# A four-layer graph network on one core: GpSimd's order at the start, a table load between two stages, and the elu ends of the last attention group moved

## The chip, the cores and the metric

The kernel runs on one core of one Trainium2 chip. The metric is device time in microseconds (us) of one execution. It is launched once and computes everything on the core. Engines are TensorE (PE), VectorE (DVE), ScalarE (ACT), GpSimd (POOL) and SyncE (SP), which issues most of the transfers.

## The reference, cut to what matters

There are N = 1250 nodes of 1024 features and E = 20000 edges (src, dst, edge_weight), sorted by dst. Four layers are applied, each as x = x + layer(relu(layernorm(x))):

```
edge_index = stack([src, dst])
x = x + L0(h)   # x1 = h @ W1 + b1 (1024 -> 512); four gated rounds:
                # deg = in-degree; dis = max(deg, 1) ** -0.5
                # alpha = tanh(x_i @ gw[:512] + x_j @ gw[512:] + gb)
                # out += segment_sum(dis[row] * dis[col] * alpha * x_j, col)
                # result is concat([x1, out])
x = x + L1(h)   # W = zeros(1024, 1024).at[row, col].add(edge_weight); h @ W.T + bias
x = x + L2(h)   # graph convolution with self loops: relu(A_norm (h @ W) + b)
x = x + L3(h)   # h = h @ W; e = exp(-leaky_relu(al[src] + ar[dst]))
                # h' = segment_sum(e * h[dst], src) / (rowsum + 1e-5)
                # elu(h')
```

## The kernel before

Nodes are padded to 1280 and worked in T = 10 tiles of 128. Matrix products run in fp32r; each left or right operand is split into a high part and a remainder (`_hi` by ScalarE, `_lo` by VectorE), and TensorE does three products (hi x hi, hi x lo, lo x hi).

**Layer 0, first part (0 to 123 us).** For every tile, `x1_pe` multiplies with W1. Between the steps of this product TensorE builds the matrix of edge counts and the matrix of edge weights: edges are picked into windows of five nodes with one-hot matrices (`pick_edges`), then `cells` (VectorE) makes one-hot operands for 25 groups, `cells_pe` multiplies them and `take_cells` (ScalarE) copies them out. `place_pe`, `place_act` and `place_dve` say which group is handled at which of four places in a tile; these orders are written out by hand. `transpose_pe` turns the normalised input, `transposed_act` and `transposed_dve` split it into `hT_hi` and `hT_lo`.

GpSimd makes the layernorm factor of a pair of tiles with `scale_pool(i)`, six instructions on 128x2 values (L532 to L542), because the power function there keeps ScalarE's table alone. It also splits the edge weights into three bf16 parts (`ew_part`, five instructions on 80x250 values, L844 to L852), which `pick_edges` needs for its last six products (L1787). ScalarE's `place_bias(0)` (L1008) writes the bias times the factor into the bank of the first product; TensorE's first product waits for it. ScalarE also makes `w1_hi` for eight rows of blocks (L1029) and VectorE `w1_lo` (L1411). The edges' ends and weights are then blended by VectorE (L1309 to L1336), and ScalarE's `widen_parts` (L1045, `ew_ids`) makes them ready for `cells`.

**From layer 0's first part to the gated rounds (112 to 125 us).** VectorE computes `norm` from the degrees; ScalarE takes its root (`norm_root`, L1093), VectorE makes `dis` from it (L1493 to L1501). A dummy Tanh on ScalarE (L1095) stands behind the root. `gates(t, ..)` (L1391, L1394, VectorE) makes the two gate values of a tile. `spread_u` (L1866, TensorE) puts `u` on all partitions. Then for every tile s of a half: `tanh` (ACT, L1110), `mask_of` (DVE, L1508), `mask_hi_of` (ACT, L1115), `mask_rest` (DVE, L1513), and 15 products (L1972 to L1974) on TensorE. `g_split` (ACT, L1099) and `g_rest` (DVE, L1399) split g. `take_x1(t)` (L996) copies x1 of tile t.

**Layers 1 and 2 (404 to 730 us)** are not touched.

**Layer 3, attention (845 us to the end).** Five groups of two destination tiles; for each group ten steps s: `logits`, `att_of` (L1688), `att_rest` (L1693) on VectorE, `exps` and `att_hi_of` on ScalarE, `sum_e` (L944 to L950) on GpSimd, 12 products on TensorE (`gat_step`, L2052). `att_rest(s)` waits for `sum_e(s)`. The group's result is finished during the next group: `gat_take` and `elu_act` on ScalarE, `elu_start` at s == 4 and `elu_end` (L1714, L1718) at s 7 and 8 on VectorE. `elu_end` adds the residual in `xres[j]` and leaves the result there.

SyncE has one queue in this stage, in this order for each of two buffers: wait for `gat_added`, store `xres[j]` to the output (L796), wait until the store has landed, load the next residual tile into the same buffer (L792):

```
def store3(i, b):
    settled(sp, gat_added, 2 * i + b + 1)
    sp.dma_start(out[rows(2 * i + b), :], xres[b][:, :]).then_inc(gat_stored[b], 16)
    settled(sp, gat_stored[b], 16 * (i + 1))
with sp.Fori(0, HT - 1) as i:
    for b in range(2):
        store3(i, b)
        load3(i + 1, b)
```

So the residuals of tiles 8 and 9 are loaded only when tiles 6 and 7 have been finished and stored. The last tile is finished in two halves of 512 columns; L1764 and L1767 are the second half's last instructions on VectorE, L1277 and L1278 ScalarE's, and L810 stores both halves.

Of the kernel before, what the change touches and what calls it, by code (L numbers as in the profile page):

```python
# [59 lines left out]
SLOTS = 5  # L60
TANH_LEAD = 3
AL_FIRST = T - 2
SCALES_AHEAD = {0: 1, 1: 2, 4: 3, 7: 4}
LAST_SUMS = (2, 3, 4, 0, 1)
EARLY = 3
TAIL = 3
# [9 lines left out]
def build_program(nc, x, src, dst, edge_weight, w1, b1, gate_w, gate_b, bias1, w2, b2, w3, att, out):  # L76
# [738 lines left out]
    def _(pool):  # L815
# [19 lines left out]

        pool.wait_ge(src_landed, 16)
        nc.gpsimd.tensor_copy(src_h[0:EDGE_ROWS, :, :], src_rows[0:EDGE_ROWS, :, :]).then_inc(src_ready, 1)
        pool.wait_ge(firsts_done, 1)
        scale_pool(pool, 0)
        pool.wait_ge(ew_landed, 16)  # L840
        ew_whole = ew_rows[0:EDGE_ROWS, :, :].rearrange("p t c -> p (t c)")
        part = [ew_part[0:EDGE_ROWS, n, :] for n in range(3)]
# [8 lines left out]
        pool.wait_ge(parts_chain, 4)  # L851
        nc.gpsimd.tensor_copy(part[2], left_over[1]).then_inc(parts_chain, 1)  # L852

        for a in range(T):
            if a in SCALES_AHEAD:
                scale_pool(pool, SCALES_AHEAD[a])
            pool.wait_ge(count_row_ready, a + 1)
            pool.dma_start(count_dram[a * P:(a + 1) * P, :], count_row[a % 2][:, :]).then_inc(count_stored[a % 2], 16)
            if a < WT_TILES:
                pool.wait_ge(weights_copied, a + 1)  # L860
                pool.dma_start(wt_dram[a * P:(a + 1) * P, :], weight_row[a % 2][:, :]).then_inc(weights_stored[a % 2], 16)
# [98 lines left out]
    def _(act):  # L960
# [50 lines left out]
        def place_act(t, place):  # L1011

            for n in groups_at(t, place, 0):
                take_cells(n)
            for a in tiles_behind(t, place, 1):
                if a < WT_TILES:
                    take_weight_rows(a)
            for a in tiles_behind(t, place, 2):
                take_count_rows(a)
# [2 lines left out]
        transposed_act(act, d, 0, 0)  # L1022
        h_act(act, d, 0, 1)
        for k in range(KT):
            if k == 2:
                place_bias(0)
            if k % 2 == 0:
                act.wait_ge(w_landed[k // 2], 16)
            nc.scalar.activation(w1_hi[:, k, :], w1_raw[:, k, :], ACT.Copy).then_inc(w_hi_ready, 1)  # L1029
# [18 lines left out]
        for t in range(T):  # L1048
            if t + 1 < T:
                transposed_act(act, d, (t + 1) // 2, (t + 1) % 2)  # L1050
            place_act(t, 0)
            if t > 0:
                take_x1(t - 1)
            place_act(t, 1)
            if t + 2 < T:
                h_act(act, d, (t + 2) // 2, t % 2)
            if t + 1 < T and t % 2 == 0:
                place_bias(t + 1)
            if t == 0:
                widen_rows()  # L1060
                widen_parts()
            if t == FIRST_STEP:
                act.wait_ge(complete_ready, 1)
                whole = act.value_load(complete[0:1, 0:1], min_val=0, max_val=1)
            place_act(t, 2)
            if t + 1 < T and t % 2 == 1:
                place_bias(t + 1)
            place_act(t, 3)

        with act.If(whole == 0):  # L1070
            act.wait_ge(count_row_ready, T)
# [19 lines left out]

        act.wait_ge(norm_chain, 2)
        nc.scalar.activation(norm_root[:, :, :], norm[:, :, :], ACT.Sqrt).then_inc(norm_root_ready, 1)  # L1093

        nc.scalar.activation(rden[:, 0, 0:1], zeros[:, 0:1], ACT.Tanh).then_inc(tanh_idle, 1)  # L1095


        def g_split(t):
# [13 lines left out]
        def mask_hi_of(q, s):  # L1112
            k = s % SLOTS
            act.wait_ge(mask_ready, T * q + s + 1)
            nc.scalar.activation(mask_hi[k][:, :], mask[k][:, :], ACT.Copy).then_inc(mask_hi_ready, 1)  # L1115
# [35 lines left out]
        act.wait_ge(product_read[0], 1)  # L1151
        g_split(0)
        act.wait_ge(count_stored[0], 16 * HT)
        tanh(0, 0, 0, 1)
        mask_hi_of(0, 0)
        act.wait_ge(product_read[1], 1)
        g_split(1)
        act.wait_ge(product_ready[0], HT)
# [109 lines left out]
        with act.Fori(1, GROUPS - 1) as grp:  # L1268
            attention_act(grp, range(T), False, False)
        attention_act(GROUPS - 1, range(T), False, True)  # L1270
        gat_take(T - 2, 0)
        elu_act(T - 2, 0)
        gat_take(T - 1, 1, slice(0, HID))
        elu_act(T - 1, 1, slice(0, HID))
        end = slice(HID, D)
# [6 lines left out]
    def _(dve):  # L1282
# [130 lines left out]
        for t in range(T):  # L1413
# [22 lines left out]
                whole = dve.value_load(complete[0:1, 0:1], min_val=0, max_val=1)  # L1436
            if t == T - 2:
                gates(4, 4)
            place_dve(t, 2)
            place_dve(t, 3)  # L1440
            if t == T - 3:
# [126 lines left out]
                if h == 1 and s >= HT:  # L1568
                    g_rest(s - HT, T * nxt + s - HT)

        gates(5, 5)
        dve.wait_ge(counts_copied, CELL_GROUPS)
        mask_of(0, 0, 0)
        g_rest(0, 0)
# [145 lines left out]
        def attention_dve(grp, steps, first, last):  # L1720

            for s in steps:
                if s < T - 2:
                    logits(grp, s + 2)
                elif not last:
                    if s == T - 2 and not first:
                        dve.wait_ge(al_all_ready, 2)
                    logits(grp + 1, s + 2 - T)
                if s < T - 1:
                    att_of(grp, s + 1)  # L1730
                elif not last:
                    att_of(grp + 1, 0)
                att_rest(grp, s)
                if not first and s == 4:
                    for j in range(GRP):
                        elu_start(GRP * (grp - 1) + j, j)
                if not first and s in (7, 8):
                    elu_end(GRP * (grp - 1) + s - 7, grp - 1, s - 7)

        def attention_start():  # L1740
            dve.wait_ge(al_ready, AL_FIRST)
# [380 lines left out]
```

## Time and profile before

| | |
|---|---|
| time, median of 3 runs | 1001.96 us (1000.94 to 1003.04) |
| the profiled execution | 1001.58 us, its span 1000.0 us |
| TensorE busy | 977.4 us, 98% of the span |
| VectorE, ScalarE, GpSimd busy | 668.7, 430.9, 140.4 us |
| chain that ended last | PE 91%, DVE 5%, ACT 2%, issue 1%, POOL 1% |

The span is the time in which the profiler saw the core work; 1.58 us of the profiled execution lie around it. The chain that ended last is followed back from the last instruction, each time to what released the instruction. Starts are us from the beginning of the span.

### The profile page before, as it was taken

The page shows a single profiled execution, that of the slowest core. Times are in us where ns is not written, and L with a number is a line of the kernel's source. Part 1 is how long each engine was busy: PE and PEld are TensorE (multiplying, and loading weights), DVE is VectorE, ACT ScalarE, POOL GpSimd, SP SyncE. Part 2 cuts the span into 40 slices and gives each one's busy share as a digit, 9 for nine tenths or more (in the row PEclk, how much of TensorE's full clock was granted, in tenths as well). Part 3 has the DMA queues.
Part 4 walks back from the last instruction along what each step waited for, and adds up shares of the span by engine and source line. Part 5 has one row for each costly group of instructions (what it writes and reads, how often), then busy time and mean ns, then how long its engine had stood idle before and what let it go on. Part 6 is the DMA issues. An engine that isn't in the chain of part 4 may idle for free.

```text
span 1000.0 us, 14720 instructions
## 1 busy us (share of the span) xinstructions
PE 977.4 (98%) x5170; PEld 809.6 (81%) x5170; DVE 668.7 (67%) x1221; ACT 430.9 (43%) x650; POOL 140.4 (14%) x191
## 2 busy tenths in 40 slices
PE   5999999999999999999999999999999999999997
PEld 3788788888888888888888888888888888888886
DVE  7877888788778879354485343216446664988886
ACT  5688865554543646112242322233222232445543
POOL 3022500000000010232221000000110000333331
PEclk9999999999999999999999999999999999999999
DMA  7256580000000014745433111243451230101223
GB/s 251 101 177 222 136 255 1 1 22 0 0 21 0 0 12 104 178 171 188 180 124 116 42 42 43 77 155 106 156 180 69 69 121 0 43 22 64 84 84 122
DMA packets 27326, 93.42 MB, mean 93 GB/s; under 512 B 3530, under 2 KB 3530, under 8 KB 27136
## 3 DMA queue, kind: packets, MB, share of 16 engines
q1 hardware_dynamic: 16400, 58.07, 16.5%
q0 software_dynamic: 10880, 34.74, 11.4%
q8 instruction: 29, 0.48, 0.2%
q14 instruction: 17, 0.14, 0.0%
HBM read 64.48 MB, written 33.56 MB: 98 GB/s over the span
## 4 chain that ended last, share of the span: by engine, by line
PE 91%; DVE 5%; ACT 2%; issue 1%; POOL 1%; DMA 0%; ACTq 0%; DVEq 0%; POOLq 0%
PE ps L592 32%; PE ps L2052 11%; PE ps L1972 9%; PE ps L1974 9%; PE ps L1973 9%; PE ps L2025 5%; PE ps L2024 5%; PE ps L575 3%; PE ps L1895 1%; PE ps L1897 1%; PE ps L1896 1%; PE ps L1866 1%; PE ps L1822 1%; PE ps L1825 1%; PE ps L1838 1%
## 5 line engine op out<-in xcount | busy, mean ns | idle before, releaser
L1972 PE MATMUL ps<-g_hi,mask_hi 128*128 128x512 f32 x400 | 157.4, 394 | 2.1 <-DVE mask_lo L1513 2.1
L1974 PE MATMUL ps<-g_hi,mask_lo 128*128 128x512 f32 x400 | 155.9, 390 | 0.0
L1973 PE MATMUL ps<-g_lo,mask_hi 128*128 128x512 f32 x400 | 155.7, 389 | 0.0
L558 ACT ACTIVATE hT_hi<-ps 128x1024 fp32r<-128x1024 f32 x40 | 41.0, 1025 | 200.3 <-PE ps L575 200.3
L592 PE MATMUL ps<-w_hi,hT_hi 128*128 128x512 f32 x320 | 126.4, 395 | 0.0
L592 PE MATMUL ps<-w_lo,hT_hi 128*128 128x512 f32 x320 | 124.7, 390 | 0.0
L2052 PE MATMUL ps<-y_all,att_hi 128*128 128x512 f32 x400 | 110.0, 393 | 1.5 <-DVE att_lo L1693 1.5
L1110 ACT ACTIVATE mask<-ps,v 128x640 f32<-128x640 f32 x80 | 63.4, 793 | 111.2 <-PE ps L1974 52.9
L592 PE MATMUL ps<-w_hi,hT_lo 128*128 128x512 f32 x320 | 98.6, 389 | 0.0
L1972 PEld LDWEIGHTS ps<-g_hi,mask_hi 128*128 128x128 f32 x400 | 75.1, 188 | 20.4 <-DVE mask_lo L1513 3.3
L2052 PEld LDWEIGHTS ps<-y_all,att_hi 128*128 128x128 f32 x400 | 74.0, 188 | 17.3 <-DVE att_lo L1693 1.5
L1974 PEld LDWEIGHTS ps<-g_hi,mask_lo 128*128 128x128 f32 x400 | 75.1, 188 | 16.0
L1973 PEld LDWEIGHTS ps<-g_lo,mask_hi 128*128 128x128 f32 x400 | 75.1, 188 | 15.1
L565 DVE TENSOR_TENSOR hT_lo<-ps,hT_hi 128x1024 fp32r<-128x1024 f32 x40 | 48.9, 1222 | 46.3 <-ACT hT_hi L558 46.3
L1508 DVE TENSOR_TENSOR mask<-mask,countT 128x640 f32<-128x640 f32 x80 | 65.5, 819 | 14.2 <-ACT mask L1110 14.2
L592 PEld LDWEIGHTS ps<-w_hi,hT_lo 128*128 128x128 f32 x320 | 60.1, 188 | 12.8
L592 PEld LDWEIGHTS ps<-w_lo,hT_hi 128*128 128x128 f32 x320 | 60.2, 188 | 11.8
L592 PEld LDWEIGHTS ps<-w_hi,hT_hi 128*128 128x128 f32 x320 | 60.1, 188 | 11.9
L1513 DVE TENSOR_TENSOR mask_lo<-mask,mask_hi 128x640 fp32r<-128x640 f32 x80 | 65.3, 818 | 0.4 <-ACT mask_hi L1115 0.3
L1115 ACT ACTIVATE mask_hi<-mask 128x640 fp32r<-128x640 f32 x80 | 58.8, 735 | 15.3 <-DVE mask L1508 15.0
L592 PE MATMUL ps<-wt_hi,hT_hi 128*128 128x512 f32 x160 | 63.3, 396 | 0.0
L2052 PE MATMUL ps<-y_all,att_lo 128*128 128x512 f32 x200 | 63.3, 390 | 0.0
(203 smaller groups left out, 1839.2 us busy)
## 6 DMA issues: line engine op xcount, KB each, us to landing
xin<-x_after SPq DMA_DIRECT2D x30, 512.0 KB, 3.3
xres<-x_after POOLq DMA_DIRECT2D x20, 512.0 KB, 4.2
x_after<-xres POOLq DMA_DIRECT2D x20, 512.0 KB, 3.0
w_raw<-in_L_gnn_W SPq DMA_DIRECT2D x8, 1024.0 KB, 7.2
x_after<-g POOLq DMA_DIRECT2D x20, 256.0 KB, 7.4
xres<-x_after SPq DMA_DIRECT2D x10, 512.0 KB, 3.4
xin<-in_x SPq DMA_DIRECT2D x9, 512.0 KB, 3.4
out_x<-xres SPq DMA_DIRECT2D x9, 512.0 KB, 2.7
```

Source lines behind the costliest of these rows:

```text
L565: nc.vector.tensor_tensor(hT_lo[b][:, :, :].rearrange("p k m -> p (k m)"), TRANSPOSED, hT_hi[b][:, :, :].rearrange("p k m -> p (k m)").bit ...
L592: last = nc.tensor.matmul(PRODUCT[d.n][b][:, half * BANK:(half + 1) * BANK], left[:, k, :], right[:, k, half * BANK:(half + 1) * BANK], st ...
L1110: nc.scalar.activation(mask[k][:, :], U_ALL, ACT.Tanh, bias=v[:, s:s + 1]).then_inc(tanh_ready, 1)
L1115: nc.scalar.activation(mask_hi[k][:, :], mask[k][:, :], ACT.Copy).then_inc(mask_hi_ready, 1)
L1508: nc.vector.tensor_tensor(mask[k][:, :], mask[k][:, :], countT[:, s, h * HALF:(h + 1) * HALF], ALU.mult).then_inc(mask_ready, 1)
L1513: nc.vector.tensor_tensor(mask_lo[k][:, :], mask[k][:, :], mask_hi[k][:, :].bitcast(F32), ALU.subtract).then_inc(mask_lo_ready, 1)
L1972: nc.tensor.matmul(SUMS[dd], mask_hi[k][:, cols], g_hi[:, s, :], start=(s == 0), stop=False)
L1973: nc.tensor.matmul(SUMS[dd], mask_hi[k][:, cols], g_lo[:, s, :], start=False, stop=False)
L1974: last = nc.tensor.matmul(SUMS[dd], mask_lo[k][:, cols], g_hi[:, s, :], start=False, stop=(s == T - 1))
L2024: nc.tensor.matmul(out_n, left, y_hi[s][:, n * BANK:(n + 1) * BANK], start=(s == 0), stop=False)
L2025: last = nc.tensor.matmul(out_n, left, y_lo[s][:, n * BANK:(n + 1) * BANK], start=False, stop=(s == T - 1))
L2052: last = nc.tensor.matmul(AGG[j][:, n * BANK:(n + 1) * BANK], left, right[:, n * BANK:(n + 1) * BANK], start=(s == 0 and len(rights) == 2 ...
```

## The change

Five things are changed.

- On GpSimd the five instructions on the edge weights now stand ahead of `scale_pool(0)`. On ScalarE `place_bias(0)` moves from ahead of the third block of `w1_hi` to ahead of the seventh.
- ScalarE runs a dummy Sqrt in step t = 8 of the first part, behind `place_act(8, 3)`. The dummy Tanh behind the root is removed. (That `place_act(t, 0)` changes sides with `take_x1(t - 1)` at t = 9 moves no instruction: no group and no tile falls on that place.)
- ScalarE's `mask_hi_of(0, 0)` comes ahead of `tanh(0, 0, 0, 1)`.
- VectorE's `gates(5, 5)` moves from behind `dis` to step t = 8, ahead of `norm`.
- In the last attention group VectorE runs both `elu_end` behind the ten steps and no longer at s 7 and 8. ScalarE's last `gat_take`s wait for `gat_added`, since they overwrite `gat_sums`.

```
-        pool.wait_ge(firsts_done, 1)
-        scale_pool(pool, 0)
         pool.wait_ge(ew_landed, 16)
...
         nc.gpsimd.tensor_copy(part[2], left_over[1]).then_inc(parts_chain, 1)
+        pool.wait_ge(firsts_done, 1)
+        scale_pool(pool, 0)
...
         for k in range(KT):
-            if k == 2:
+            if k == 6:
                 place_bias(0)
...
             place_act(t, 3)
+            if t == T - 2:
+                nc.scalar.activation(rden[:, 0, 1:2], zeros[:, 0:1], ACT.Sqrt).then_inc(tanh_idle, 1)
...
         nc.scalar.activation(norm_root[:, :, :], norm[:, :, :], ACT.Sqrt).then_inc(norm_root_ready, 1)
-        nc.scalar.activation(rden[:, 0, 0:1], zeros[:, 0:1], ACT.Tanh).then_inc(tanh_idle, 1)
...
+        mask_hi_of(0, 0)
         tanh(0, 0, 0, 1)
-        mask_hi_of(0, 0)
...
+        act.wait_ge(gat_added, T - GRP - 1)
         gat_take(T - 2, 0)
         elu_act(T - 2, 0)
+        act.wait_ge(gat_added, T - GRP)
         gat_take(T - 1, 1, slice(0, HID))
...
             if t == T - 2:
                 gates(4, 4)
+                gates(5, 5)
...
-        gates(5, 5)
         dve.wait_ge(counts_copied, CELL_GROUPS)
         mask_of(0, 0, 0)
...
-                if not first and s in (7, 8):
+                if not first and not last and s in (7, 8):
                     elu_end(GRP * (grp - 1) + s - 7, grp - 1, s - 7)
+            if last:
+                for j in range(GRP):
+                    elu_end(GRP * (grp - 1) + j, grp - 1, j)
```

## Rows read from the trace of the kernel before

**Rows 1.** Timeline of GpSimd, 9 to 17 us: start, duration, what [idle before, releaser]

```profile
9.22 0.73 POOL L532 TENSOR_TENSOR rough<-variance,minus_half 128x2 f32<-128x2 f32 x1 [1.72 <-DVE variance L506]
...
11.27 0.39 POOL L844 CAST ew_part<-ew_rows 80x250 bf16<-80x250 f32 x1
...
12.46 2.00 POOL L848 CAST ew_part<-ew_rest 80x250 bf16<-80x250 f32 x1
...
15.55 0.73 POOL L852 CAST ew_part<-ew_rest 80x250 bf16<-80x250 f32 x1
```

**Rows 2.** The transfer of the edge weights: issue, and us from issue to landing

```profile
L687 SPq DMA_DIRECT2D ew_rows<-in_edge_weight x1: 441/441/441, 3.4 to 3.4; - x1
...
DMA to landing us min/median/max: 6.6/6.6/6.6
```

**Rows 3.** Timeline of ScalarE, 12 to 29 us

```profile
12.82 0.68 ACT L1008 ACTIVATE ps<-b_all,bias_scale 128x512 f32<-128x512 f32 x1
...
13.43 3.21 ACT L1029 ACTIVATE w_hi<-w_raw 128x512 fp32r<-128x512 f32 x6
...
27.90 1.46 ACT L1045 ACTIVATE ew_ids<-edges 125x1500 bf16<-125x1500 f32 x1
```

**Rows 4.** Timeline of VectorE, 12 to 32 us

```profile
12.93 5.71 DVE L1411 TENSOR_TENSOR w_lo<-w_raw,w_hi 128x512 fp32r<-128x512 f32 x8
...
21.90 1.23 DVE L565 TENSOR_TENSOR hT_lo<-ps,hT_hi 128x1024 fp32r<-128x1024 f32 x1 [0.39 <-ACT hT_hi L558]
...
26.11 1.08 DVE L1336 COPY_PREDICATED edges<-here,ps 125x250 f32<-125x250 int32 x3
...
30.31 1.22 DVE L565 TENSOR_TENSOR hT_lo<-ps,hT_hi 128x1024 fp32r<-128x1024 f32 x1 [1.32 <-ACT hT_hi L558]
```

**Rows 5.** Timeline of ScalarE: the first table load, and 116 to 121 us

```profile
1.03 1.28 ACT L551 ACT_TABLE_LOAD   x1 [1.03 <-PEq L2112]
...
116.48 0.69 ACT L996 ACTIVATE g<-ps,scale 128x512 f32<-128x512 f32 x1 [1.49 <-PE ps L1897]
117.19 1.28 ACT L1093 ACT_TABLE_LOAD   x1
...
120.12 0.78 ACT L1110 ACTIVATE mask<-ps,v 128x640 f32<-128x640 f32 x1
```

**Rows 6.** ScalarE's queue: the waits ahead of the first tanhs, ns, 100 to 130 us

```profile
L1109 ACTq EVENT_SEMAPHORE  x6: 17/28/2115, 116.8 to 129.8; - x6
```

**Rows 7.** Timeline of VectorE, 118 to 127 us

```profile
118.73 0.28 DVE L1493 RECIPROCAL dis<-norm_root 128x20 f32<-128x20 f32 x1 [3.31 <-ACT norm_root L1093]
...
119.91 0.69 DVE L1391 CUSTOM_DVE_ANT_0 gate_scratch<-g,gw 128x512 f32<-128x512 f32 x1
...
125.44 0.82 DVE L1513 TENSOR_TENSOR mask_lo<-mask,mask_hi 128x640 fp32r<-128x640 f32 x1 [0.27 <-ACT mask_hi L1115]
```

**Rows 8.** Timeline of TensorE: the first product of the gated rounds

```profile
123.92 0.47 PE L1972 MATMUL ps<-g_hi,mask_hi 128*128 128x512 f32 x1 [0.88 <-DVE mask_lo L1513]
```

**Rows 9.** Timeline of TensorE in the last attention group

```profile
984.06 1.19 PE L2052 MATMUL ps<-y_all,att_hi 128*128 128x512 f32 x4 [1.12 <-DVE att_lo L1693]
```

**Rows 10.** Timeline of VectorE, 993 to 997 us

```profile
993.44 0.69 DVE L1714 SCALAR_TENSOR_TENSOR elu_neg<-elu_neg,xres 128x512 f32<-128x512 f32 x1 [0.77 <-ACT elu_neg L1236]
...
995.88 0.69 DVE L1764 SCALAR_TENSOR_TENSOR elu_neg<-elu_neg,xres 128x512 f32<-128x512 f32 x1 [0.69 <-ACT elu_neg L1277]
```

**Rows 11.** Timeline of GpSimd in the last attention group

```profile
975.37 0.74 POOL L946 TENSOR_TENSOR e_part<-e_part,att_e 128x256 f32<-128x256 f32 x1 [0.89 <-DVE att_e L1688]
```

**Rows 12.** Timeline of SyncE's queue, 980 to 989 us

```profile
980.43 0.35 SPq L796 DMA_DIRECT2D out_x<-xres  x1
983.33 0.34 SPq L792 DMA_DIRECT2D xres<-x_after  x1
...
988.83 0.34 SPq L792 DMA_DIRECT2D xres<-x_after  x1
```

**Rows 13.** Landing of the six loads of L792, 925 to 1000 us

```profile
DMA to landing us min/median/max: 3.1/3.4/4.0
```

More of the change, by code:

```diff
@@ L62 @@
 AL_FIRST = T - 2
-SCALES_AHEAD = {0: 1, 1: 2, 4: 3, 7: 4}
+SCALES_AHEAD = {0: (1,), 1: (2,), 4: (3,), 7: (4,)}
 LAST_SUMS = (2, 3, 4, 0, 1)
@@ L837, in _ @@
         nc.gpsimd.tensor_copy(src_h[0:EDGE_ROWS, :, :], src_rows[0:EDGE_ROWS, :, :]).then_inc(src_ready, 1)
-        pool.wait_ge(firsts_done, 1)
-        scale_pool(pool, 0)
         pool.wait_ge(ew_landed, 16)
@@ L852, in _ @@
         nc.gpsimd.tensor_copy(part[2], left_over[1]).then_inc(parts_chain, 1)
+        pool.wait_ge(firsts_done, 1)
+        scale_pool(pool, 0)
         for a in range(T):
-            if a in SCALES_AHEAD:
-                scale_pool(pool, SCALES_AHEAD[a])
+            for i in SCALES_AHEAD.get(a, ()):
+                scale_pool(pool, i)
             pool.wait_ge(count_row_ready, a + 1)
@@ L1024, in _ @@
         for k in range(KT):
-            if k == 2:
+            if k == 6:
                 place_bias(0)
@@ L1050, in _ @@
                 transposed_act(act, d, (t + 1) // 2, (t + 1) % 2)
-            place_act(t, 0)
+            if t < T - 1:
+                place_act(t, 0)
             if t > 0:
                 take_x1(t - 1)
+            if t == T - 1:
+                place_act(t, 0)
             place_act(t, 1)
@@ L1068, in _ @@
             place_act(t, 3)
+            if t == T - 2:
+                nc.scalar.activation(rden[:, 0, 1:2], zeros[:, 0:1], ACT.Sqrt).then_inc(tanh_idle, 1)
         with act.If(whole == 0):
@@ L1093, in _ @@
         nc.scalar.activation(norm_root[:, :, :], norm[:, :, :], ACT.Sqrt).then_inc(norm_root_ready, 1)
-        nc.scalar.activation(rden[:, 0, 0:1], zeros[:, 0:1], ACT.Tanh).then_inc(tanh_idle, 1)
         def g_split(t):
@@ L1153, in _ @@
         act.wait_ge(count_stored[0], 16 * HT)
+        mask_hi_of(0, 0)
         tanh(0, 0, 0, 1)
-        mask_hi_of(0, 0)
         act.wait_ge(product_read[1], 1)
@@ L1270, in _ @@
         attention_act(GROUPS - 1, range(T), False, True)
+        act.wait_ge(gat_added, T - GRP - 1)
         gat_take(T - 2, 0)
         elu_act(T - 2, 0)
+        act.wait_ge(gat_added, T - GRP)
         gat_take(T - 1, 1, slice(0, HID))
@@ L1438, in _ @@
                 gates(4, 4)
+                gates(5, 5)
             place_dve(t, 2)
@@ L1569, in half_dve @@
                     g_rest(s - HT, T * nxt + s - HT)
-        gates(5, 5)
         dve.wait_ge(counts_copied, CELL_GROUPS)
@@ L1736, in attention_dve @@
                         elu_start(GRP * (grp - 1) + j, j)
-                if not first and s in (7, 8):
+                if not first and not last and s in (7, 8):
                     elu_end(GRP * (grp - 1) + s - 7, grp - 1, s - 7)
+            if last:
+                for j in range(GRP):
+                    elu_end(GRP * (grp - 1) + j, grp - 1, j)
         def attention_start():
```

## The prediction

> **What bounds the kernel.** I read the page first. TensorE is busy for 98% of the span and makes nine tenths of the chain that ended last, so an edit pays only where TensorE or that chain waits for what is edited. I then read the chain in order of time. It leaves TensorE in three places, and the change touches these three: the start, up to about 43 us, where it runs over GpSimd, ScalarE and VectorE; the step into the gated rounds at 117 to 124 us; and the last attention group. For each I read the timelines of all engines. The reader should look in [rows 1, 3, 4] for who waits for whom at the start, in [rows 5 to 8] for the 0.88 us in which TensorE is idle before the first gated product, and in [rows 9 to 13] for its 1.12 us in the last group and for the store-and-load chain of SyncE beside it. Middle layers are unchanged and a shift at one place is carried to the end, since TensorE is the bound between them.
>
> **A. The start.** GpSimd makes the factor from 9.22 to 11.27 (2.05 us) and the parts from 11.27 to 16.28 (5.01 us) [rows 1]. The parts can't start before the weights have landed, at 3.4 + 6.6 = 10.0 us [rows 2], so they start 1.2 us earlier and not 2.05. A cast costs 0.39 alone, 0.73 beside VectorE's `w_lo` and once 2.00, when it met the start of that series [rows 1, 4]. With all three casts at 0.39 the five instructions take 5.01 - 1.61 - 0.34 = 3.06 us; done at 13.1. If the last cast, which now falls on 12.4 to 12.5, meets the same 2.0 us, they are done at 14.7. The factor follows: 2.05 us alone, and with 0.34 more for each of six instructions beside `w_lo` 4.1 us. I call its end S. At the ends S = 13.1 + 2.05 = 15.2 and 14.7 + 4.1 = 18.8. I take 17.4: parts done at 13.9, halfway, and 3.5 us for the factor, nearer to the contended row because `w_lo` runs until at least 16.6 (six of 0.62 from 12.93).
>
> What waits for S: `place_bias(0)` now stands ahead of the last two of `w1_hi`. Behind S come the bias (13.43 - 12.82 = 0.61), two `w1_hi` (3.21 / 6 = 0.535 each), one `w1_lo` (about 0.68), and some 0.1 between engines [rows 3, 4]: `w1_lo` ends at S + 2.5. It ended at 18.64 before, so VectorE is late by S - 16.1. Queued behind it on VectorE are the next tile's statistics, the blends and `hT_lo(1)`. Two slacks take something back: 0.39 us of idle ahead of `hT_lo(1)`, and 27.90 - 27.19 = 0.71 us by which the blended weights were ready before ScalarE came to widen them, because it had been held by a bank that TensorE opens; TensorE's earlier picks remove that hold [rows 3, 4]. From there `ew_ids`, `hT_hi(2)` and `hT_lo(2)` follow one another, and VectorE waited 1.32 us for this [rows 4], then ran without a gap into the 43 us mark. So the shift is S - 16.1 - 1.1 = S - 17.2, and no less than -1.1. With S = 17.4 it is **+0.2**; the bounds are -1.1 and +1.6.
>
> A rule of the Trainium skill bears here (SBUF — State Buffer, "Who interferes with whom"): VectorE with two SBUF inputs and a reading GpSimd exclude each other for a whole instruction. The casts of 0.39, 0.73 and 2.00 us agree in kind. By this rule each small instruction would wait for the end of a `w_lo`, some 4 us for the factor, and the sum would be about 0.6 us higher.
>
> **B. Into the gated rounds.** Two table loads stand between `take_x1(8)` and the first tanh: 117.19 to 120.12 [rows 5]. The Sqrt load moves into ScalarE's idle time ahead of 116.48, 1.49 us long; load and dummy take 1.28 + 0.2 = 1.48. That is covered, by a hair; each 0.1 us more would delay `take_x1(8)` by as much. The root then runs at 117.2 and `dis` comes 1.3 us earlier. `gates(5, 5)`, 1.4 us, now stands ahead of `norm`: VectorE was idle 3.31 us waiting for the root [rows 7], of which the load is 1.28 and the rest, 2.0, covers it. Where does the Tanh load go? The queue waits for the spread u from 116.8 for 2.115 us, to 118.9 [rows 6]. The very first load ran at 1.03 us [rows 5], ahead of its activation's wait for statistics of an input that was only being issued then. If this load goes ahead of its waits too, it runs from 117.4 to 118.7 and is hidden, and the first tanh starts at 118.9 instead of 120.12. From there tanh 0.7, `mask_of` 0.75 (no gates ahead of it), `mask_hi` 0.7 (no tanh ahead of it), `mask_lo` 0.8: ready at 122.1. But TensorE is in the last x1 product until 123.92 - 0.88 = 123.04 [rows 8], and nothing moves that. So 1.9 us of earlier masks are worth **-0.9**. The next step keeps it: `take_x1(9)` waits for the same product's end and stands ahead of `mask_hi(1)`, so it too comes 0.9 earlier. Bounds: -0.9, and +0.3 (the third rival).
>
> A second rule speaks against this edit: ScalarE: Activation LUTs, "What ACT_TABLE_LOAD costs", puts a switch at 1.28 us of load and 1.38 us of drain. The trace has two loads, a root and a dummy in 2.93 us [rows 5], which two such switches would not fit into. By the rule the load would reach 1.2 us beyond the idle time and the sum would be about 0.8 us higher.
>
> **C. The end.** TensorE waits 1.12 us for `att_lo` of step 9, because VectorE runs two `elu_end` between steps 7 and 9 [rows 9]. With them behind, the operand is ready long before: -1.1 for TensorE's end. But what is late next is the transfers. `elu_end(6)` now waits for `att_rest(9)`, which waits for two sums on GpSimd, 0.74 each and some 0.3 between [rows 11]: 2 x 1.05 + 0.35 = 2.4 us later; free of GpSimd's reads it is some 0.4 faster. So the store of tile 6 goes from 980.43 to 982.4. Its buffer is loaded 2.9 us later, the other buffer's load follows 5.5 us behind that (983.33, 988.83 in [rows 12]), so at 990.8; it lands 3.1 to 4.0 us later [rows 13], at 993.9 to 994.8. The first half of the last tile needs it; it ran at 993.44 and would be ready at 992.3. VectorE's last instructions had 0.69 us of idle at 995.88 [rows 10], so a landing at L moves the end by L - 993.44 - 0.69: at 994.5, **+0.4**. Bounds: -1.1, if a load waits only for a lone store of 2.9 us and no landing is late, and +0.8, a 4.0 landing with 0.1 to wake. ScalarE's new wait for `gat_added` of tile 6 (982.2) is over before the last step's products, which start at 982.9 and which it needs anyway: no cost.
>
> **Sum.** +0.2 - 0.9 + 0.4 = -0.3 against the profiled execution's own 1001.58 (span 1000.0 and 1.58 around it): 1001.3. The median of the runs is 0.4 above that execution, so 1001.6 to 1001.7; I give 1001.6.
>
> **Rivals.**
> 1. *The last load is in time.* For it: it was so in [rows 12] with the store 2 us earlier, and the loads spread by 0.9 us. Against: SyncE issues one after the other. C = -1.1: total -1.8, 1000.2; with a factor at its earliest (A = -1.1) -3.1, 998.9.
> 2. *The factor becomes the bound (slower than before).* GpSimd's six small instructions each wait out a `w_lo`, place: `place_bias(0)`, S = 18.8. For it: the 2.00 us cast. Against: `w_lo` runs dry by 17 us, and GpSimd is then alone. A = +1.6: total +1.1, 1003.1. Beyond S = 17.7 the whole change is slower than before.
> 3. *The Tanh load stands behind its wait.* For it: this activation has two waits and the one at 1.03 us had one. Then it runs 118.9 to 120.2, tanh is not earlier; the first product is 0.6 earlier by order alone, but `mask_hi(1)`, now behind two tanhs and `take_x1(9)`, ends at 125.7 against 125.4 [rows 7], and VectorE sets the pace there. B = +0.1: total +0.7, 1002.7.
> 4. *The preload doesn't do what it says*, since a branch lies between it and the root and the table is loaded again, or it costs more than its 1.49 us: B about 0: +0.6, 1002.6.
>
> **Chances.** Forecast 0.42, first rival 0.2 (a quarter of it with the early factor), second 0.13, third 0.15, fourth 0.1. Bounds together: -1.1 - 0.9 - 1.1 = -3.1 and +1.6 + 0.3 + 0.8 = +2.7; with the median, 998.9 and 1004.7. The range 999.2 to 1003.6 leaves out only joint extremes. 0.2% is 2.0 us, about what a measurement of this kernel can tell from no change. Only the first rival's early part and the better half of its rest pass it downwards: 0.15; the second with a late landing upwards: 0.06; within 0.2%: 0.79.
>
> **What would show it.** A: `ew_part` starts near 10.05, `bias_scale` ends near 17.4, `hT_lo(2)` near 30.5. B: one table load near 115.0, one near 117.4, no idle of TensorE ahead of L1972, which starts 0.9 earlier relative to A's shift. C: no idle of TensorE in the last group, the second load of L792 near 990.8 and VectorE's L1714 on 512 columns waiting for it. Wrong would be: a factor done before 16, a Tanh load at 118.9, or a residual that lands before 993.

## The result: 1004.3 us, 0.2% slower, where 1001.6 was forecast

The changed kernel takes 1004.30 us (median of 17 runs, 1002.83 to 1005.97) beside 1002.14 us for the kernel before on the same chip; the ratio is 1.0019, with a 95% interval of 1.0012 to 1.0026. That is 2.2 us slower, at the bound of 2.0 us that the prediction called measurable, above its range (to 1003.6). The prediction gave 0.79 to a change within 0.2% and 0.06 to a slower kernel; the measured change lies on the border of the two, the ratio just inside and the difference of the medians just outside. The profiled execution took 1004.52 us, with a span of 1003.0.

The span was followed at marks that both kernels have. Each line gives the start of one instruction before and after:

| mark | before | after | shift | gained or lost since the last |
|---|---|---|---|---|
| `hT_lo(2)` on VectorE (end of A) | 30.31 | 32.18 | +1.87 | +1.87 |
| first gated product on TensorE | 123.92 | 125.80 | +1.88 | 0.0 |
| second spread of u on TensorE (end of B) | 148.23 | 150.78 | +2.55 | +0.67 |
| last group's first row sums on TensorE | 963.88 | 966.47 | +2.59 | +0.04 |
| last product of TensorE | 994.66 | 995.83 | +1.17 | -1.42 |
| last instruction of VectorE (end of C) | 996.60 | 999.63 | +3.03 | +1.86 |

So in the profiled executions A cost 1.87 where +0.2 stood in the sum, B cost 0.67 where -0.9 stood, and C cost 3.03 - 2.59 = 0.44, where +0.4 stood. (The first mark is known less well than its digits say: in the five profiled executions of kernels that keep the old start, `b_alone` to `best1` below, it lies between 29.58 and 31.00.) Between the marks of B and C nothing moved, as the prediction had it.

**The start.** GpSimd's timeline in the changed kernel, 10 to 19 us, which answers to [rows 1]:

```profile
10.64 0.39 POOL L842 CAST ew_part<-ew_rows 80x250 bf16<-80x250 f32 x1 [2.10 <-DMA ew_rows<-in_edge_weight]
...
11.84 0.39 POOL L846 CAST ew_part<-ew_rest 80x250 bf16<-80x250 f32 x1
...
13.00 3.91 POOL L850 CAST ew_part<-ew_rest 80x250 bf16<-80x250 f32 x1
16.88 0.73 POOL L532 TENSOR_TENSOR rough<-variance,minus_half 128x2 f32<-128x2 f32 x1
17.68 0.19 POOL L534 TENSOR_TENSOR square<-rough 128x2 f32<-128x2 f32 x1
...
18.79 0.20 POOL L542 TENSOR_TENSOR bias_scale<-scale,variance 128x2 f32<-128x2 f32 x1
```

VectorE's timeline beside it, 12 to 33 us, which answers to [rows 4]:

```profile
12.97 3.69 DVE L1416 TENSOR_TENSOR w_lo<-w_raw,w_hi 128x512 fp32r<-128x512 f32 x6
20.38 1.29 DVE L1416 TENSOR_TENSOR w_lo<-w_raw,w_hi 128x512 fp32r<-128x512 f32 x2 [3.73 <-ACT w_hi L1029]
...
32.18 1.23 DVE L565 TENSOR_TENSOR hT_lo<-ps,hT_hi 128x1024 fp32r<-128x1024 f32 x1 [0.68 <-ACT hT_hi L558]
```

And the bias on ScalarE's timeline, which answers to [rows 3]:

```profile
19.11 0.69 ACT L1008 ACTIVATE ps<-b_all,bias_scale 128x512 f32<-128x512 f32 x1 [3.36 <-POOL bias_scale L542]
```

Read the three together. The weights' parts do start early, but the third cast takes 3.91 us instead of the 0.39 of the two before it: it begins 0.03 us behind the first `w_lo` and ends 0.25 us behind the sixth. So the parts are done at 16.91, later than before (16.28), and the factor comes behind them, at 18.99. ScalarE waits 3.36 us for it ahead of the seventh `w1_hi`, and VectorE 3.73 us for that one.

**Into the gated rounds.** ScalarE's timeline, 116 to 123 us, answers to [rows 5], and the line under it, from its queue (count: min/median/max ns of waiting), to [rows 6]:

```profile
116.95 1.28 ACT L1073 ACT_TABLE_LOAD   x1
118.24 0.20 ACT L1073 ACTIVATE rden<-zeros 128x1 f32<-128x1 bf16 x1
118.40 0.69 ACT L996 ACTIVATE g<-ps,scale 128x512 f32<-128x512 f32 x1
118.99 0.21 ACT L1098 ACTIVATE norm_root<-norm 128x20 f32<-128x20 f32 x1
120.91 1.28 ACT L1113 ACT_TABLE_LOAD   x1 [1.71 <-issue]
122.21 0.80 ACT L1113 ACTIVATE mask<-ps,v 128x640 f32<-128x640 f32 x1
...
L1112 ACTq EVENT_SEMAPHORE  x5: 17/17/1982, 118.9 to 129.6; - x5
```

The Sqrt load is hidden: `take_x1(8)` starts at 118.40, and 116.48 plus the shift of 1.88 would be 118.36. The Tanh load isn't: ScalarE stands idle for 1.71 us while its queue waits for the spread of u from 118.9 for 1.98 us, and the table is loaded only then. TensorE's timeline at the first gated products, which answers to [rows 8]:

```profile
125.80 0.47 PE L1980 MATMUL ps<-g_hi,mask_hi 128*128 128x512 f32 x1 [0.83 <-DVE mask_lo L1519]
...
133.26 0.47 PE L1980 MATMUL ps<-g_hi,mask_hi 128*128 128x512 f32 x1 [0.42 <-DVE mask_lo L1519]
```

The idle of 0.88 us has become 0.83, and another of 0.42 stands behind it. The way from `take_x1(8)` to the first gated product is as long as before (7.40 us against 7.44), so the missed load took away a gain and lost nothing. The 0.67 us are lost behind that product: from it to the second spread of u it takes 24.98 us, before 24.31. Two lines show where, the first from ScalarE's timeline, the second from VectorE's:

```profile
124.05 0.74 ACT L1118 ACTIVATE mask_hi<-mask 128x640 fp32r<-128x640 f32 x1 [0.44 <-DVE mask L1514]
128.01 0.82 DVE L1519 TENSOR_TENSOR mask_lo<-mask,mask_hi 128x640 fp32r<-128x640 f32 x1 [0.96 <-ACT mask_hi L1118]
```

With `mask_hi_of(0, 0)` ahead of the second tanh, ScalarE stands idle for 0.44 us until `mask_of` is done; in the kernel before it made that tanh in the meantime. Now two tanhs and not one stand between the first `mask_hi` and the second, which start 3.18 us apart instead of 2.51. So the second `mask_lo` starts 2.21 us behind the first gated product and no longer 1.52 (125.44 in [rows 7]).

**The end.** In the last group TensorE no longer waits for `att_lo`; the 1.12 us of [rows 9] are gone. The view of waits (total us, times, longest) of the whole execution has one such wait left, and it ends at 864.96, in the first group:

```profile
PE ps L2060 <- DVE att_lo L1698: 0.4, 1, 0.4
```

VectorE's timeline, 992 to 1001 us, answers to [rows 10]:

```profile
992.14 1.23 DVE L1719 SCALAR_TENSOR_TENSOR elu_neg<-elu_neg,xres 128x1024 f32<-128x1024 f32 x1 [3.09 <-DMA xres<-x_after]
...
997.12 0.69 DVE L1719 SCALAR_TENSOR_TENSOR elu_neg<-elu_neg,xres 128x512 f32<-128x512 f32 x1 [1.71 <-DMA xres<-x_after]
...
999.63 0.69 DVE L1775 TENSOR_TENSOR xres<-elu_neg,gat_sums 128x512 f32<-128x512 f32 x1
```

SyncE's timeline, 985 to 994 us, answers to [rows 12]:

```profile
985.20 0.35 SPq L796 DMA_DIRECT2D out_x<-xres  x1
988.09 0.34 SPq L792 DMA_DIRECT2D xres<-x_after  x1
988.77 0.35 SPq L796 DMA_DIRECT2D out_x<-xres  x1
993.55 0.34 SPq L792 DMA_DIRECT2D xres<-x_after  x1
```

The load that must wait for the store goes out at 988.09, the next one 5.46 us behind it, and VectorE, free since TensorE's products came earlier, waits 3.09 and 1.71 us for the two to land.

### The profile page after: what moved, and what is told of

Read it like the earlier page. It is cut to its first block, busy times and chain, and to the rows that moved or that the text cites. A ratio compares the mean times of both kernels' runs of the same rounds, so it can differ in the third digit from the quotient of the medians.

```text
span 1003.0 us, 14723 instructions
## 1 busy us (share of the span) xinstructions
PE 978.5 (98%) x5170; PEld 810.3 (81%) x5170; DVE 667.4 (67%) x1221; ACT 431.5 (43%) x650; POOL 140.1 (14%) x191
## 4 chain that ended last, share of the span: by engine, by line
PE 86%; DVE 8%; ACT 2%; issue 2%; DMA 1%; POOL 1%; SPq 0%; ACTq 0%; DVEq 0%; POOLq 0%
PE ps L592 32%; PE ps L2060 10%; PE ps L1980 8%; PE ps L1982 8%; PE ps L1981 8%; PE ps L2033 5%; PE ps L2032 5%; PE ps L575 3%; PE ps L1903 1%; PE ps L1905 1%; PE ps L1904 1%; DVE wt_lo L490 1%; PE ps L1830 1%; PE ps L1833 1%; PE ps L1874 1%
```

## The experiments

Theory T: A's loss is the third cast, shut out by VectorE's series; B's is the Tanh load behind its wait; C's is the chain of stores and loads. Rival theories were that the three parts disturb one another, that the factor's small instructions are slow beside `w_lo`, and that late weights explain A. First each part alone. `a_alone` has the change's edits on GpSimd and ScalarE's `k == 6`, `b_alone` those of the table, of `mask_hi_of(0, 0)` and `gates(5, 5)`, `c_alone` those of the last group, as in the diff above. The fourth is `b_alone` with the removed dummy put back:

```
+                nc.scalar.activation(rden[:, 0, 1:2], zeros[:, 0:1], ACT.Sqrt).then_inc(tanh_idle, 1)
...
         nc.scalar.activation(norm_root[:, :, :], norm[:, :, :], ACT.Sqrt).then_inc(norm_root_ready, 1)
         nc.scalar.activation(rden[:, 0, 0:1], zeros[:, 0:1], ACT.Tanh).then_inc(tanh_idle, 1)
...
+        mask_hi_of(0, 0)
         tanh(0, 0, 0, 1)
-        mask_hi_of(0, 0)
```

> Only the edits at the start: the edge weights' parts ahead of the norm factor on GpSimd, the bias of the first product ahead of the seventh block of w1_hi. Theory 1 (the last cast is shut out by VectorE's series of w_lo, and the bias, the last w_hi and w_lo wait for the factor): the cast takes 3 to 4 us and ends with the sixth w_lo, the factor is done at 19.0, hT_lo(2) starts 1.9 us later than before (30.31), and the time is about 1.9 us above before. Rival (the 3.9 us cast was chance in one execution, or comes from the late landing of the weights): the cast is back at 0.4 to 2.0 us, the factor is done by 17.4 and the time is within 0.5 us of before.

> Only the edits at the step into the gated rounds: Sqrt table loaded in idle time, dummy Tanh removed, mask_hi ahead of the second tanh, gates(5, 5) ahead of norm. Theory 1 (the Tanh load stands behind the wait for the spread u): load at about 119.0 to 120.3, first tanh at 120.3, TensorE idle 0.7 to 0.9 us ahead of the first gated product and again within the half; +0.7 us over before. Rival (the load comes late only because the start is late): first tanh at 118.9, -0.9 us.

> The same edits, but the dummy Tanh behind the root stays. Theory 1 (a dummy with no wait in front lets the load run during the wait for the spread u): load at 117.4 to 118.7, first tanh at 118.9 to 119.0, no idle of TensorE ahead of the first gated product; -0.9 us against before, and 1.6 us below the same edits without the dummy. Rival (the loss in these edits comes from the order of mask_hi and tanh or from gates(5, 5), not from the load): the first tanh is early but TensorE still idles; +0.2 to +0.7 us.

> Only the edit at the end: both elu_end of the last group behind its ten steps. Theory 1 (TensorE gains 1.1 to 1.3 us, and the residual of the last tile, loaded through store, load, store, load, lands later than it is needed): TensorE's last product ends 1.2 us earlier than before, VectorE waits for the last load, the end comes 0.4 us later than before. Rival (the loads were late only by chance): the last load lands by 992.5, the end is 1.1 us earlier.

| kernel | us | ratio to before | what the stage showed |
|---|---|---|---|
| `a_alone` | 1003.23 | 1.0014 [1.0005, 1.0023] | factor done at 17.95, `hT_lo(2)` +0.83 |
| `b_alone` | 1002.38 | 1.0008 [0.9999, 1.0017] | `take_x1(8)` to the second spread 32.38, before 31.75: +0.63 |
| `b_tanh_kept` | 1001.37 | 0.9995 [0.9986, 1.0004] | the same stretch 31.40: -0.35 |
| `c_alone` | 1002.32 | 1.0004 [0.9995, 1.0013] | last product -1.4, VectorE's last instruction +0.06, both beside the stage's start |

With 1001.89 for before, the three parts cost 1.34, 0.49 and 0.43 us; together 2.26, where the whole costs 2.16. They add up within what these medians tell (each of the three ratios is known to 0.0009, some 0.9 us), and the marks agree for B: +0.63 alone, +0.67 in the whole. So nothing speaks for a mutual disturbance. For A and C the single parts cost less at their marks than in the changed kernel: 0.83 and 0.06 us against 1.87 and 0.44. Of the single ratios only that of A is clear of 1; for B and C the rows of the stage decide. In `a_alone` the third cast took 2.59 us, less than the 3 to 4 that theory 1 expected and more than the rival's 2.0 at most; it ends 0.25 us behind the fourth `w_lo`, where the next `w_hi` had come only 0.04 us before:

```profile
12.84 2.59 POOL L850 CAST ew_part<-ew_rest 80x250 bf16<-80x250 f32 x1
15.39 1.17 POOL L532 TENSOR_TENSOR rough<-variance,minus_half 128x2 f32<-128x2 f32 x1
```

For B, ScalarE's timeline in `b_alone`, where the load stands behind the idle time:

```profile
116.86 0.21 ACT L1095 ACTIVATE norm_root<-norm 128x20 f32<-128x20 f32 x1
118.79 1.28 ACT L1111 ACT_TABLE_LOAD   x1 [1.71 <-issue]
```

and in `b_tanh_kept`, where it follows the root at once and is over when the spread of u comes:

```profile
117.98 0.21 ACT L1095 ACTIVATE norm_root<-norm 128x20 f32<-128x20 f32 x1
118.21 1.28 ACT L1097 ACT_TABLE_LOAD   x1
...
119.92 0.80 ACT L1112 ACTIVATE mask<-ps,v 128x640 f32<-128x640 f32 x1 [0.22 <-issue]
```

From `take_x1(8)` to the first gated product it is 6.40 us here, 7.40 in `b_alone` and 7.44 before. The dummy without a wait is what places the load, and it is worth 1.0 us. But -0.9 was expected of `b_tanh_kept` and -0.35 came: ScalarE again stands idle ahead of the first `mask_hi`, 0.72 us here, and from the first gated product to the second spread it takes 25.00 us, before 24.31. So 0.69 of the 1.04 us are lost again, and by the rows it is the new order of `mask_hi` and tanh that loses them: the first two `mask_hi` start 3.19 us apart, before 2.51. No run has that order alone. For C, VectorE's waits in `c_alone`, 980 to 1004 us:

```profile
DVE elu_neg L1716 <- DMA xres<-x_after: 4.4, 2, 2.8
```

The second group asks what in A costs, and what C is worth without the chain. `a_gated` is `a_alone` with the first `w1_lo` held until the parts are done. `a_bias_late` keeps GpSimd's old order and moves only the bias. `c_own` is `c_alone` with buffers of their own for the residuals of the last two tiles, loaded at the start of the attention, so that no load waits for a store. `best1` is before with B (Tanh kept) and `c_own`.

```
a_gated:
         transposed_dve(dve, d0, 0, 0)
+        dve.wait_ge(parts_chain, 5)
         for k in range(KT):
a_bias_late:
-            if k == 2:
+            if k == 6:
                 place_bias(0)
c_own:
+    xlast = [at(f"xlast{b}", [P, D], F32, R_X + (24 + 4 * b) * KIB) for b in range(2)]
...
         load3(0, 1)
+        for b in range(2):
+            sp.dma_start(xlast[b][:, :], x3_dram[rows(T - 2 + b), :]).then_inc(copy_landed, 16)
-        with sp.Fori(0, HT - 1) as i:
+        with sp.Fori(0, HT - 2) as i:
...
-        elu_end(T - 2, GROUPS - 1, 0)
+        elu_end(T - 2, GROUPS - 1, 0, res=xlast)
```

> The edits at the start alone, and VectorE's series of w_lo waits in addition until the weights' parts are made. Theory 1 (w_lo shuts the last cast out): all three casts take 0.39 us, the parts are done 2.4 us after the weights have landed (near 12.9), w_lo starts right behind that instead of at 12.7; the shut-out can then hit the factor's first instruction, so its end is between 15.5 and 18.5, and the time is 0 to 1.3 us above before. Rival (the cast is long by itself or by a transfer): it still takes 2.6 to 3.9 us, w_lo starts only at 15.5 or later and the time is 3 us or more above before.

> Only the place of the first product's bias on ScalarE (ahead of the seventh block of w1_hi and not of the third); GpSimd's order as before, so the factor is ready at 11.3 and nobody waits for it. Theory 1 (the loss at the start comes from the factor's lateness alone): same time as before within 0.3 us. Rival (the place of the bias costs by itself, since TensorE's first product waits for it): its first product starts later and the time is 0.5 us or more above before.

> The edit at the end alone, and the residuals of tiles 8 and 9 get buffers of their own, loaded at the start of the attention; the store of tiles 6 and 7 holds up no load. Theory 1 (the late residual eats TensorE's gain): TensorE's last product ends 1.2 us earlier than before, VectorE waits for no transfer in the last group, the end comes 1.1 to 1.3 us earlier than before, 1.6 us below the edit alone. Rival (the end is bound by the elu chain itself, behind two elu_end on VectorE): the end moves by less than 0.4 us from before.

> The start as before; the middle edits with the dummy Tanh kept; the end with own buffers for the last residuals. Theory 1 (the three places add up): -0.35 us for the middle (as its trace gave within the stage) and -1.2 us for the end, together -1.6 us against before, ratio 0.9985, and 3.5 us below the changed kernel. Rival (an earlier end only moves a wait into the last stores): within 0.5 us of before.

| kernel | us | ratio to before | what the stage showed |
|---|---|---|---|
| `a_gated` | 1003.23 | 1.0012 [1.0003, 1.0021] | factor done at 17.2, `hT_lo(2)` +0.09 |
| `a_bias_late` | 1002.36 | 1.0008 [0.9998, 1.0017] | `hT_lo(2)` +3.35 in the profiled execution |
| `c_own` | 1000.32 | 0.9986 [0.9978, 0.9995] | no wait for a transfer, VectorE ends at 994.86 |
| `best1` | 1000.44 | 0.9985 [0.9976, 0.9993] | first gated product 122.72, VectorE ends at 994.59 |

GpSimd's timeline in `a_bias_late`, and under it VectorE's line beside it:

```profile
12.92 3.86 POOL L848 CAST ew_part<-ew_rest 80x250 bf16<-80x250 f32 x1
16.86 1.13 POOL L850 TENSOR_TENSOR ew_rest<-ew_rest,ew_part 80x250 f32<-80x250 f32 x1
```

```profile
12.85 3.69 DVE L1411 TENSOR_TENSOR w_lo<-w_raw,w_hi 128x512 fp32r<-128x512 f32 x6
```

Here GpSimd's order is the old one, and the cast is shut out all the same, now the second one. So the order alone isn't the cause, and neither theory of this run had foreseen it: TensorE waits here for the parts (5.07 us, before 2.48) and not for the bias. With the bias ahead of the third `w1_hi`, ScalarE is 0.6 us late with it, and the third `w_lo` has to wait or nearly so. In `b_alone`, whose start is the old one, it starts 0.06 us behind the end of the second `w_lo`, and the cast ends 0.25 us behind that end; in the kernel before there is no idle time to be seen, but the third `w_hi` is ready only 0.16 us before the second `w_lo` ends, and the cast (the 2.00 of [rows 1]) ends again 0.25 us behind it. With the bias at the seventh block every `w_hi` of the six is ready earlier (0.20 us or more here, 0.22 or more in the changed kernel), the six `w_lo` follow one another, and the cast waits for all of them. The margins are tenths, and the runs of this kernel fit a matter of chance, though only one of them was profiled: of its nine runs at a mean granted clock of 0.999 five took 1001.05 to 1001.43 and four 1004.41 to 1005.19, some 3.5 us apart, about the 3.35 that `hT_lo(2)` was late in the profiled one (1004.86).

GpSimd's timeline in `a_gated`:

```profile
13.03 0.39 POOL L850 CAST ew_part<-ew_rest 80x250 bf16<-80x250 f32 x1
...
14.18 0.61 POOL L534 TENSOR_TENSOR square<-rough 128x2 f32<-128x2 f32 x1
```

The cast is back at 0.39, though ScalarE and the transfers do what they did in `a_alone`: it is VectorE's series that shuts it out. A's shift is almost gone; the parts are done at 13.4, and the factor's last five instructions, which now meet the `w_lo`, take 0.51 to 0.61 each instead of 0.20. Its median is no better than that of `a_alone`, though. From `hT_lo(2)` to the first gated product it takes 94.86 us, where before took 93.61 and `a_alone` 94.98; the last section comes to that.

The third group takes the order apart from the place of the bias, and makes the best of both. `a_order` has GpSimd's new order and the bias at `k == 2`. `a_bias_gate3` has the old order, the bias at `k == 6` and `dve.wait_ge(parts_chain, 3)` ahead of the first `w1_lo`. `after_mended` is the changed kernel with the dummy Tanh and the buffers of `c_own`. `best2` is `best1` with that wait for 3.

> Only GpSimd's order is changed (parts ahead of the factor); the first product's bias stays ahead of the third block of w1_hi. Theory 1 (the last cast is shut out as long as VectorE's w_lo follow without a gap; the bias at the third block holds up w1_hi and so opens a gap after two of them): the cast takes 1 to 2 us and not 3.9, the factor is done near 16.5 to 17, but six w1_hi and six w_lo now wait for it, so the last w_lo ends near 22 and the time is 2.5 to 4 us above before. Rival (order alone decides how long the cast is): it takes 2.6 to 3.9 us as in the changed kernel, factor at 18 to 19.

> The bias at the seventh block, GpSimd's order as before, and VectorE's first w_lo waits until the second cast (the one that took 3.86 us with the late bias) is done. Theory 1 (the late bias costs only because six w_lo follow without a gap and shut that cast out): the cast takes 0.39 us, w_lo starts at 13.3, the parts are done by 15.2 and not at 18.8, and the time is that of before within 0.4 us or up to 0.5 us below. Rival (the late bias itself costs): the time stays 0.8 us above before.

> The changed kernel with two of its parts mended: the dummy Tanh is kept, and the residuals of tiles 8 and 9 have buffers of their own. Theory 1 (the three places are independent): 1.4 us for the start, -0.35 for the middle, -1.3 for the end, so 0.2 us below before, within 0.5 us; 2.2 us below the changed kernel. Rival (the late start also sets the later places): 1 us or more above before.

> The start as before with one wait more (VectorE's first w_lo waits for the second cast of the parts), the middle edits with the dummy Tanh kept, the end with own buffers. Theory 1 (a cast that isn't shut out makes the parts 1.1 us earlier for 0.4 us of w_lo): -0.3 us against the same without the wait, ratio 0.998 against before. Rival (VectorE's later w_lo takes it all back): 0.9985, as without the wait, or above.

| kernel | us | ratio to before | what the stage showed |
|---|---|---|---|
| `a_order` | 1004.88 | 1.0027 [1.0016, 1.0038] | factor done at 16.3, `hT_lo(2)` +1.61 |
| `a_bias_gate3` | 1002.38 | 1.0002 [0.9993, 1.0011] | cast 0.39, `hT_lo(2)` -0.82 |
| `after_mended` | 1001.49 | 0.9994 [0.9985, 1.0003] | cast 4.22, `hT_lo(2)` +1.62, VectorE ends at 996.55 |
| `best2` | 1000.00 | 0.9981 [0.9972, 0.9990] | `hT_lo(2)` -0.67, VectorE ends at 994.28 |

GpSimd's and VectorE's timelines in `a_order`:

```profile
12.64 1.61 POOL L850 CAST ew_part<-ew_rest 80x250 bf16<-80x250 f32 x1
...
17.72 3.70 DVE L1411 TENSOR_TENSOR w_lo<-w_raw,w_hi 128x512 fp32r<-128x512 f32 x6 [3.72 <-ACT w_hi L1029]
```

The cast came in here, at 1.61 us, and yet A is dear: the bias, at its old place, now waits for a factor that comes at 16.3 and holds six of the eight blocks. So the halves of A lose by different ways: the order because the factor is late, which alone costs more (2.8 us) than both halves together in `a_alone` (1.3); the place of the bias because it closes the gap, which happened in the profiled execution, while its median isn't clear of before. `a_bias_gate3` shows the other side; with 0.64 us of waiting on VectorE the cast takes its 0.39. The same in `best2`:

```profile
12.70 0.39 POOL L856 CAST ew_part<-ew_rest 80x250 bf16<-80x250 f32 x1
...
14.37 0.74 POOL L860 CAST ew_part<-ew_rest 80x250 bf16<-80x250 f32 x1
...
13.13 5.53 DVE L1424 TENSOR_TENSOR w_lo<-w_raw,w_hi 128x512 fp32r<-128x512 f32 x8 [0.24 <-POOL ew_part L856]
```

The second line is the cast that comes next. It begins within a series of eight `w_lo` without an idle time and takes 0.74 us all the same, as it does in `a_bias_gate3`. So a series without a gap doesn't shut out whatever comes: it did so only to the cast that was under way or began between 0.47 us ahead of the first `w_lo` and 0.15 us behind it. Why is open.

`best2` beats both kernels: 1.9 us below before by its ratio, 4.3 below the changed one by the medians. That its one wait more is worth something isn't shown: its ratio and that of `best1` lie within each other's intervals, and its `hT_lo(2)` at 29.64 is among those of the old start (29.58 to 31.00). `after_mended`, which keeps the whole of A, can't be told from before; against `best1`, which differs from it by A alone, its `hT_lo(2)` is 1.85 us later and its end 1.96. It also settles the theory of the late weights. In it they landed as early as in the kernel before, 6.6 us after their issue, the cast began 0.27 us ahead of the first `w_lo`, and it was shut out longest. The landing, the cast on GpSimd and the series on VectorE:

```profile
DMA to landing us min/median/max: 6.6/6.6/6.6
...
12.45 4.22 POOL L858 CAST ew_part<-ew_rest 80x250 bf16<-80x250 f32 x1
...
12.72 3.69 DVE L1423 TENSOR_TENSOR w_lo<-w_raw,w_hi 128x512 fp32r<-128x512 f32 x6
```

## Why the prediction was wrong, by its own steps

**A, the third cast (failed; most of the error).** The step "if the last cast meets the same 2.0 us" took the dearest cast of the old trace as the dearest that there can be. When it meets the start of a `w_lo` series without a gap it takes 3.86 to 4.22 us (`a_bias_late`, the changed kernel, `after_mended`). The prediction saw that the bias moves from the third block to the seventh, and costed it on ScalarE alone; it didn't ask what the 0.6 us of bias did to VectorE's series. The bound S = 18.8 was passed by 0.2. The rest of the step held: S - 17.2 gives 1.8 for S = 18.99 (measured 1.87), 0.75 for the 17.95 of `a_alone` (0.83) and 0.0 for the 17.2 of `a_gated` (0.09). That the agreement is within 0.1 is in part luck, since the mark itself spreads by more in the kernels with the old start.

**The second rival came true in its S, with another mechanism.** S was 18.99 where it had 18.8, and that it came so near is luck: the parts were done 2.2 us later than its 14.7, and the factor took 2.1 us and not 4.1. Its cause, six small instructions that each wait out a `w_lo`, wasn't: the first took 0.73, as it did before, and the other five 0.19 to 0.20 each, since VectorE by then stood idle, waiting for what the factor held up. As to the rule of the Trainium skill (SBUF — State Buffer, "Who interferes with whom"), exclusion for a whole instruction fits `a_gated`, 0.51 to 0.61 each beside `w_lo` of 0.62. But the cast of 3.91 us beside 3.69 us of `w_lo` was kept out over six instructions, not one.

**The landing of the weights (not the cause).** They landed 7.2 us after their issue instead of 6.6, so the parts began at 10.64 and not at 10.05. That didn't decide: with a landing of 6.6 the cast was shut out too (`after_mended`). Over the profiled executions the landing was 6.6 to 7.6, so a step that hangs on tenths can't be read from one trace.

**B, the Tanh load (failed).** The step "if this load goes ahead of its waits too" is refuted by 120.91 in the changed kernel and 118.79 in `b_alone`: it stands behind the wait, as the third rival had it. The load at 1.03 us was the wrong model, as that rival's own argument said. The rival's +0.1 was too small as well, against 0.63 in `b_alone`: the first product didn't come 0.6 earlier by order but stayed where it was, as the first tanh came 0.2 later and ScalarE then stood idle for 0.44. Once the load was placed, the way to the first product was as forecast: in `b_tanh_kept` it is 1.04 shorter than before (0.9 forecast).

**B, "the next step keeps it" (failed).** Of these 1.04 us 0.35 is left at the second spread. The step counted on `take_x1(9)` alone for the second `mask_hi`; the new order put one more tanh between the first `mask_hi` and the second (3.19 us from start to start, before 2.51), and the first gained nothing by it, since ScalarE idles ahead of it for 0.72 us. The third rival named the right path (`mask_hi(1)`, VectorE sets the pace) and mis-sized it: 0.1 for 0.63. So of the 1.6 us by which B was off 1.0 is the Tanh load and 0.6 this order.

**B, the Sqrt preload (right).** Covered to within 0.04 us, with 1.28 for the load and nothing on its two sides, so the fourth rival falls. By the rule of the Trainium skill (ScalarE: Activation LUTs, "What ACT_TABLE_LOAD costs") 1.38 us of drain would have come on top; the trace disagrees, as the dummy starts at 118.24 and `take_x1(8)` at 118.40.

**C (right, by the forecast steps; the size in part by luck).** TensorE's end 1.42 earlier against 1.1 (1.12 are the idle time; the other 0.3 stays open); the second load 5.46 us behind the first against 5.5; landings of 4.0 and 3.5, inside 3.1 to 4.0; VectorE's end +0.44 against +0.4. In `c_alone`, with the same edits, the second load went out 5.25 us behind the first and landed in 3.4, and the end moved by +0.06. The first rival falls: the last load was not in time. `c_own` shows what the chain ate. Without it VectorE's end comes 1.41 us earlier than in the old kernel, both beside the stage's start.

**The sum.** A was off by 1.7, B by 1.6, C by 0.0. Both errors had the same sign, which the chances had treated as joint extremes, though both came from the same habit: a wait or a contention that the old trace doesn't show was priced by the nearest row of that trace.

## What to carry to other kernels

A small stall can be the gap another engine lives on: before a stall is removed or moved, look which engines' instructions are longer beside this series than alone, and take as the upper bound of each the whole unbroken series (3.9 to 4.2 us here for a cast of 0.39), even if it usually waits for one instruction only. The Tanh load stood right ahead of its activation and behind that activation's waits in both kernels without a dummy, though the program's first load ran ahead of one; a dummy activation that waits for nothing puts the load into an idle time (1.0 us here), and removing the dummy gives that back. An instruction that is moved ahead in its engine's order brings its own wait with it, and what it passed comes later: `mask_hi` ahead of a tanh cost 0.7 us. Work that is put behind the last tiles pays only if no load waits there for a store that this work feeds; two buffers loaded early turned +0.06 us (`c_alone`) into -1.41 (`c_own`).

## What the runs showed of the hardware that was not expected

**Who is let in.** The same GpSimd cast (80x250, 0.39 us alone) took 0.73 to 0.79 us when it was let in behind one `w_lo`, 1.38 to 2.59 us when it met the start of a series that had a gap (`a_order`, `a_alone`, before, `b_alone`, `c_alone`), and 3.86 to 4.22 us when it met the start of six `w_lo` without a gap. In every one of these it ended 0.25 us behind the end of a `w_lo`; the runs don't show why it was let in behind one and not behind another.

**The clock after a pause.** In every trace TensorE is idle for 1.7 to 2.5 us near 42 us, and in some executions the granted clock then falls. Two rows of busy time by stretch (PE, PEld, DVE, ACT, POOL, granted clock, DMA share, GB/s), first of the changed kernel, then of `a_gated`:

```profile
40.00:50.00 10.00, 8.05 (x115) 6.86 (x114) 8.86 (x16) 5.88 (x10) 0.00 (x0) 1.00 0.01 2
```

```profile
40.00:50.00 10.00, 7.48 (x94) 6.70 (x93) 7.37 (x14) 6.06 (x9) 0.00 (x0) 0.83 0.03 4
```

A mean of 0.83 is the lower level (1.2 GHz) for a third of these 10 us, the upper (2.4 GHz) for the rest. Five of the fourteen profiled executions have the fall, those of `a_alone`, `a_gated`, `a_order`, `a_bias_gate3` and `b_tanh_kept`. In them the way from `hT_lo(2)` to the first gated product is 1.2 to 1.6 us longer than in others with the same kind of step (93.6 with the Tanh load late or as before, 92.6 with the new edits and the dummy Tanh). Their mean clock over the whole execution is 0.997 or 0.998, that of the other nine 0.999 or 1.0. If this sign holds for the executions without a profile, the difference of the medians is between 0.4 us (the changed kernel) and 1.7 (`a_bias_gate3`); in `a_alone` seven such runs have a median of 1003.48 and the other four of 1001.99. It isn't equally frequent: 25 of 97 runs of the kernel before, 13 of 55 with the old start (`b_alone`, `b_tanh_kept`, `c_alone`, `c_own`, `best1`), but 7 of 11 for `a_alone`, 8 of 11 for `a_gated` and `a_bias_gate3` each, 7 of 7 for `a_order` and 13 of 17 for the changed kernel; 5 of 11 for `after_mended` and `best2` each and 3 of 12 for `a_bias_late`. It can add to what A costs the median of the changed kernel, whose profiled execution hasn't got it. It doesn't explain why the median of `a_gated` is no better than that of `a_alone`: both profiled executions have the fall, and there `a_gated` is 0.70 us shorter. That stays open. In `a_gated` and `a_order` the pause at the fall is 2.5 us, in the changed kernel and before 1.95 and 1.73 without a fall; but in `b_tanh_kept` the clock fell after 1.74, and in `after_mended` it stayed up after 2.37. So the length of the pause alone doesn't decide, and what does stays open.
